# Last experts stage as one stream over its chunks, and shorter gate work in the second merged LSTM and experts stage

## The reference, cut to what matters

```python
z = xz_t + prev_h @ Wh
ai, af, ao, ag = jnp.split(z, 4, axis=1)
next_c = sigmoid(af) * prev_c + sigmoid(ai) * tanh(ag)
next_h = sigmoid(ao) * tanh(next_c)
...
h = jnp.einsum('nc,ech->neh', x_flat, W1) + b1          # 16 experts, top 2
h = _layernorm(h, g1, be1)                              # rsqrt(var + 1e-5)
h = jax.nn.gelu(h, approximate=False)
expert_out = jnp.einsum('neh,eho->neo', h, W2) + b2
```

```python
h = jax.nn.gelu(jnp.einsum('bsd,edf->ebsf', x, W1) + b1[:, None, None, :], approximate=False)
eo = jnp.einsum('ebsf,efd->ebsd', h, W2) + b2[:, None, None, :]
out = jnp.einsum('ebsd,bse->bsd', eo, comb)
x = x + out
```

## Time and profile before

| what | us |
|---|---|
| median of 3 runs (4591.7 to 4593.56) | 4591.94 |
| time of the profiled execution | 4592.8 |
| its span, first to last instruction | 4591.0 |
| merged stage, 160 steps, 1427 to 2163.3 in the trace | 736.3 |
| of it the stretch with experts, 1494 to 2114 | 620 |
| last stage, from 4048.77 to the end | 542.2 |
| mean granted TensorE clock, share of full | 0.963 |

### The profile page before, as it was taken

The page is one execution under the profiler, slowest core; times in us unless marked ns, Lnnn a source line. Parts: engine busy times, 40 slices in busy tenths (PEclk is TensorE's granted clock), DMA queues, the critical chain, the costliest instruction groups (busy, mean ns, idle before and its releaser), DMA issues. The chain is left out here.

```text
span 4591.0 us, 117961 instructions
## 1 busy us (share of the span) xinstructions
PE 4209.4 (92%) x40912; PEld 2942.6 (64%) x40912; DVE 2537.7 (55%) x7670; ACT 1904.5 (41%) x4829; POOL 784.3 (17%) x3251
## 2 busy tenths in 40 slices
PE   6999999999998888898799998999996887889998
PEld 4555776887775455554355887887783555566666
DVE  5775564555554888886555445666666554421111
ACT  4343443333332555564233222666663552333333
POOL 1111221000000666663221000111112110000000
PEclk9999999999999999999799998999998998989999
DMA  1000000000000000000000000000000000000000
GB/s 54 0 0 25 0 0 26 1 0 0 0 0 11 1 2 1 1 1 1 34 0 3 0 0 1 3 3 3 3 3 13 41 0 0 0 1 0 0 0 18
DMA packets 3085, 28.94 MB, mean 6 GB/s; under 512 B 320, under 2 KB 832, under 8 KB 1216
## 3 DMA queue, kind: packets, MB, share of 16 engines
q1 hardware_dynamic: 2768, 24.97, 1.4%
HBM read 22.87 MB, written 2.10 MB: 5 GB/s over the span
## 5 line engine op out<-in xcount | busy, mean ns | idle before, releaser
L2312 DVE SCALAR_TENSOR_TENSOR experts_acc<-banks,experts_gate,experts_acc 128x128 f32<-128x128 f32 x512 | 144.2, 344 | 462.1 <-PE banks L2258 461.0
L2258 PEld LDWEIGHTS banks<-weights,experts_hidden 128*128 128x128 f32 x2560 | 303.3, 192 | 55.0 <-issue 49.7
L604 DVE TENSOR_REDUCE cells_row_max<-banks 128x4 f32<-128x512 f32 x384 | 238.5, 684 | 162.8 <-PE banks L397 162.8
L2258 PE MATMUL banks<-weights,experts_hidden 128*128 128x128 f32 x2560 | 305.2, 275 | 0.0
L2531 ACT ACTIVATE experts_hidden<-banks,weights 128x512 f32<-128x512 f32 x256 | 175.9, 687 | 271.1 <-PE banks L2528 267.2
L761 PE MATMUL banks<-clock_fill 128*128 128x512 bf16 x932 | 282.6, 392 | 1.2 <-PEq L101 1.2
L2528 PE MATMUL banks<-act_a,weights 128*128 (+1 forms) x512 | 263.4, 646 | 0.0
L541 ACT ACTIVATE cells_probs<-banks 128x512 f32<-128x512 f32 x384 | 198.3, 602 | 97.4 <-PE banks L437 90.1
L604 DVE TENSOR_REDUCE attn_row_max<-banks 128x4 f32<-128x512 f32 x256 | 159.0, 684 | 133.4 <-PE banks L397 133.4
L1579 ACT ACTIVATE wave_hidden_turned<-banks,weights 128x128 f32<-128x128 f32 x512 | 205.7, 454 | 40.4 <-PE banks L1523 37.3
L2717 ACT ACTIVATE lin_context_turned<-banks 128x256 f32<-128x256 f32 x128 | 49.2, 384 | 403.7 <-PE banks L2669 403.7
(11 more groups left out here) (528 smaller groups left out, 9909.9 us busy)
## 6 DMA issues: line engine op xcount, KB each, us to landing
weights<-in_p SPq DMA_DIRECT2D x1, 2894.5 KB, 17.2
weights<-in_p SPq DMA_DIRECT2D x1, 2894.0 KB, 9.4
...
x_res<-in_x SPq DMA_DIRECT2D x1, 2048.0 KB, 15.2
out_x<-x_res SPq DMA_DIRECT2D x1, 2048.0 KB, 6.3
...
```

The costliest lines, as they stand in the source:

```text
L604: dve.tensor_reduce(mt[:, 4 * g:4 * g + 4], bank, AX_X, ALU.max).then_inc(s["max_ready"], 1)
L2258: last = pe.matmul(ps[:, 2 + e % 2, t * P:(t + 1) * P], hs[lo:lo + n, (tile + f) % slots, t * P:(t + 1) * P], out_rhs(e, f, lo, n), start= ...
L2312: last = dve.scalar_tensor_tensor(out=acc[:, t, :], in0=ps[:, 2 + e % 2, t * P:(t + 1) * P], scalar=g[:, t, e:e + 1], in1=acc[:, t, :], op ...
```

## The change

The last stage gets a function of its own, `wide_expert_stage`. The sum, the gates and the turned gates have two buffers, by the chunk's parity. The bias is no longer put into the sum ahead of the experts: the first expert writes the sum by a multiply, and a chunk's bias product (one of 128x512 with gates in 128 rows, of which 8 are not zero) and the four products that turn its sum (now plain products with the identity) are added up in one PSUM bank during the next chunk, behind expert 1's output. Gates are turned behind expert 4's output. The hidden tiles of the next chunk's first expert are issued ahead of the last expert's output. The stage's loop takes two chunks in a pass, three times, with the first and last chunk written out. SyncE sends each chunk's 256 KB to memory when it is stored; the block behind the stage is gone.

In the merged stage `guess` is one operation on the bits. The output gate's own operation is gone: `state` is one operation over all 128 rows and 128 columns, (tanh of the gate + 1) times `tc`, where `tc` is now as wide as `hb` and zero off its blocks, so that the cell's tanh is two operations of 64 rows each. The factor 0.5 is in `half_pick`.

```diff
...
-        og, c2, fc, ic, tc = (sb(n, [P, HALF]) for n in ("output_gate", "c_twice", "fc", "ic", "tc"))
-        hb = sb("state_by_batch", [P, P])
+        c2, fc, ic = (sb(n, [P, HALF]) for n in ("c_twice", "fc", "ic"))
+        tc, hb = (sb(n, [P, 2, HALF]) for n in ("tc", "state_by_batch"))
...
-        shifted = sb("variance_shifted", [P, 2, 4], I32)
...
             def turned(st):
                 pe.wait_ge(s["batch_ready"], st.s(1))
-                pe.matmul(ps[:, STATE, 0:2 * NB], hb[:, :], const("half_pick"), start=True, stop=True).then_inc(
+                pe.matmul(ps[:, STATE, 0:2 * NB], hb[:, :, :].rearrange("p h f -> p (h f)"), const("half_pick"), start=True, stop=True).then_inc(
...
             def cell_tanh(st):
                 act.wait_ge(s["c_ready"], st.s(1))
-                act.activation(tc[:, :], c2[:, :], ACT.Tanh, scale=0.5).then_inc(s["tc_ready"], 1)
+                for half in range(2):
+                    rows = slice(half * HALF, (half + 1) * HALF)
+                    last = act.activation(tc[rows, half, :], c2[rows, :], ACT.Tanh, scale=0.5)
+                last.then_inc(s["tc_ready"], 1)
...
-            dve.memset(hb[:, :], 0.0).then_inc(s["c_set"], 1)
+            dve.memset(tc[:, :, :], 0.0).then_inc(s["c_set"], 1)
...
                 dve.scalar_tensor_tensor(out=c2[:, :], in0=fc[:, :], scalar=0.5, in1=ic[:, :], op0=ALU.mult,
                                          op1=ALU.add).then_inc(s["c_ready"], 1)
-                dve.tensor_scalar(og[:, :], th[:, 2, :], 0.5, 0.5, ALU.mult, ALU.add).then_inc(s["gate_ready"], 1)
 
             def state(st):
-                dve.wait_ge(s["gate_ready"], st.s(1))
+
                 dve.wait_ge(s["tc_ready"], st.s(1))
-                for half in range(2):
-                    rows = slice(half * HALF, (half + 1) * HALF)
-                    last = dve.tensor_tensor(hb[rows, rows], tc[rows, :], og[rows, :], ALU.mult)
-                last.then_inc(s["batch_ready"], 1)
+                dve.scalar_tensor_tensor(out=hb[:, :, :], in0=th[:, 2:3, :].broadcast_to([P, 2, HALF]), scalar=1.0,
+                                         in1=tc[:, :, :], op0=ALU.add, op1=ALU.mult).then_inc(s["batch_ready"], 1)
...
             def guess(n, q):
 
                 dve.wait_ge(s["summed"], n + 1)
-                dve.tensor_scalar(shifted[:, q % 2, :], half_var[:, q % 2, :].bitcast(I32), 1, None,
-                                  ALU.logical_shift_right).then_inc(s["shift_ready"], 1)
-                dve.wait_ge(s["shift_ready"], n + 1)
                 past(dve, s["unit_ready"], n - 1)
-                dve.tensor_scalar(inv[:, q % 2, :].bitcast(I32), shifted[:, q % 2, :], -1.0,
+                dve.tensor_scalar(inv[:, q % 2, :].bitcast(I32), half_var[:, q % 2, :].bitcast(I32), -0.5,
                                   float(0x5F3759DF - 0x400000), ALU.mult, ALU.add).then_inc(s["guess_ready"], 1)
...
+def wide_expert_stage(core, out):
+    nc, w, ps, const = core.nc, core.pack(7), core.ps, core.const
+    NE, DEPTH = 8, 4
+    PER = NE * DEPTH
+    OUT, SUM, GTURN = 2, 4, 5
+    gates = core.gate(NE)
+    with stage_scope(nc) as ctx:
+        sb = lambda n, shape: ctx.enter_context(nc.sbuf_tensor(f"experts4_{n}", shape, F32))
+        sem = lambda n: nc.alloc_semaphore("experts4_" + n)
+        hs = sb("hidden", [P, 2 * DEPTH, CHUNK])
+        acc = sb("acc", [P, 2, 4, P])
+        g = sb("gate", [P, 2, 4, NE])
+        gt = sb("gate_turned", [P, 2, CHUNK])
+        s = {n: sem(n) for n in ["set", "g_ready", "gt_done", "gt_ready", "h_done", "h_ready", "y_done", "y_added",
+                                 "sum_done", "stored", "sent"]}
+        block = ctx.enter_context(nc.Block())
+        def chunks(eng, one):
+            one(0, 0, True, False)
+            with eng.Fori(0, NCHUNK // 2 - 1) as i:
+                one(i * 2 + 1, 1, False, False)
+                one(i * 2 + 2, 0, False, False)
+            one(NCHUNK - 1, 1, False, True)
+        @block.sync
+        def _(sp):
+            for c in range(NCHUNK):
+                cols = slice(c * CHUNK, (c + 1) * CHUNK)
+                sp.wait_ge(s["stored"], c + 1)
+                sp.dma_start(out[:, cols], core.x[:, cols]).then_inc(s["sent"], 16)
+            sp.wait_ge(s["sent"], 16 * NCHUNK)
+        @block.gpsimd
+        def _(pool):
+            pool.memset(gt[:, :, :], 0.0).then_inc(s["set"], 1)
+            def one(c, p, first, last):
+                past(pool, s["y_added"], (c - 1) * NE)
+                past(pool, s["gt_done"], c - 1)
+                pool.tensor_copy(g[:, p, :, :], gates[:, bass.ds(c * 4, 4), :]).then_inc(s["g_ready"], 1)
+            chunks(pool, one)
+        @block.tensor
+        def _(pe):
+            wait_pack(pe, core, 7)
+            def hidden(c, e):
+                for f in range(DEPTH):
+                    past(pe, s["h_ready"], c * PER + (e * DEPTH + f - 1))
+                    pe.matmul(ps[:, f % 2, :], w("W1", (e * DEPTH + f) * P, P), core.a[:, tok(c * CHUNK, CHUNK)],
+                              start=True, stop=True).then_inc(s["h_done"], 1)
+            def output(c, e):
+                past(pe, s["y_added"], c * NE + (e - 1))
+                pe.wait_ge(s["h_ready"], c * PER + (e + 1) * DEPTH)
+                for t in range(4):
+                    for f in range(DEPTH):
+                        last = pe.matmul(ps[:, OUT + e % 2, t * P:(t + 1) * P],
+                                         hs[:, e % 2 * DEPTH + f, t * P:(t + 1) * P],
+                                         w("W2", (e * DEPTH + f) * P, P), start=(f == 0), stop=(f == DEPTH - 1))
+                last.then_inc(s["y_done"], 1)
+            def gates_turn(c, p):
+                pe.wait_ge(s["g_ready"], c + 1)
+                past(pe, s["gt_ready"], c)
+                for t in range(4):
+                    last = pe.transpose(ps[0:NE, GTURN, t * P:(t + 1) * P], g[:, p, t, :], const("ident"))
+                last.then_inc(s["gt_done"], 1)
+            def total(c, p):
+                pe.wait_ge(s["y_added"], c * NE + NE)
+                pe.wait_ge(s["gt_ready"], c + 1)
+                past(pe, s["stored"], c)
+                pe.matmul(ps[:, SUM, :], w("b2"), gt[:, p, :], start=True, stop=False, skip_group_check=True)
+                for t in range(4):
+                    last = pe.matmul(ps[:, SUM, t * P:(t + 1) * P], acc[:, p, t, :], const("ident"), start=False,
+                                     stop=True, skip_group_check=True)
+                last.then_inc(s["sum_done"], 1)
+            def one(c, p, first, last):
+                for e in range(NE):
+                    if e + 1 < NE:
+                        hidden(c, e + 1)
+                    elif not last:
+                        hidden(c + 1, 0)
+                    output(c, e)
+                    if e == 1 and not first:
+                        total(c - 1, 1 - p)
+                    if e == 4:
+                        gates_turn(c, p)
+                if last:
+                    total(c, p)
+            hidden(0, 0)
+            chunks(pe, one)
+        @block.scalar
+        def _(act):
+            wait_pack(act, core, 7)
+            act.wait_ge(s["set"], 1)
+            def one(c, p, first, last):
+                for e in range(NE):
+                    past(act, s["y_done"], c * NE + (e - 1))
+                    for f in range(DEPTH):
+                        j = e * DEPTH + f
+                        act.wait_ge(s["h_done"], c * PER + (j + 1))
+                        act.activation(hs[:, e % 2 * DEPTH + f, :], ps[:, f % 2, :], ACT.Gelu,
+                                       bias=w("b1", j, 1)).then_inc(s["h_ready"], 1)
+                    if e == 5:
+                        act.wait_ge(s["gt_done"], c + 1)
+                        past(act, s["sum_done"], c - 1)
+                        act.activation(gt[0:NE, p, :], ps[0:NE, GTURN, :], ACT.Copy).then_inc(s["gt_ready"], 1)
+            chunks(act, one)
+        @block.vector
+        def _(dve):
+            def add(c, p, e):
+                dve.wait_ge(s["y_done"], c * NE + (e + 1))
+                past(dve, s["y_added"], c * NE + e)
+                for t in range(4):
+                    y, gate = ps[:, OUT + e % 2, t * P:(t + 1) * P], g[:, p, t, e:e + 1]
+                    if e == 0:
+                        last = dve.tensor_scalar(acc[:, p, t, :], y, gate, None, ALU.mult)
+                    else:
+                        last = dve.scalar_tensor_tensor(out=acc[:, p, t, :], in0=y, scalar=gate, in1=acc[:, p, t, :],
+                                                        op0=ALU.mult, op1=ALU.add)
+                last.then_inc(s["y_added"], 1)
+            def store(c):
+                dve.wait_ge(s["sum_done"], c + 1)
+                xs = core.x[:, tok(c * CHUNK, CHUNK)]
+                dve.tensor_tensor(xs, ps[:, SUM, :], xs, ALU.add).then_inc(s["stored"], 1)
+            def one(c, p, first, last):
```

(23 more changed lines are left out.)

21 lines of the change are left out of this document (4 added, 17 removed).

## The result

The changed kernel takes 4521.07 us (median, 4516.34 to 4524.8), the one before 4592.75 in the same session: 0.9843, 95% interval [0.9831, 0.9855], 72 us less. Forecast were 4531, 61 less. The profiled execution has a span of 4517.4 us.

The account below looks back on a forecast made before the run. TensorE was taken as the bound, with gaps at the last stage's chunk boundaries and waits for VectorE in the merged stage. Last stage -49 and merged stage -12 make -61, so 4531 us; range 4521 to 4552, own range 4522 to 4541.

Parts of the forecast that it names:

- The bound and the mechanism of the last stage: Last stage: TensorE's work is the bound; without boundary waits the chunks form one stream at full clock, -49 us.
- The start: Last stage's beginning: hidden products start earlier, but at a low clock, which loses 3 us.
- The price of the old restart: Last stage, behind each old chunk boundary: first 16 hidden products take 10.15 us instead of 7.4, up to 2.75 us lost.
- I let 9 us of the 18.1 go: Merged stage, logits steps: 9 us of TensorE's 18.1 us of waits for VectorE's units vanish.
- 4 with the routing and the jump: Merged stage, routing steps and loop's back jump: the shorter guess saves 0.21 us a step, 4 us over some 20 stalls.
- Tanh and state cancel: Merged stage, steps without experts: split tanh +0.16 us (bounds 0.12 and 0.26), single state operation -0.16, sum 0.
- my dear end: Merged stage, cell tanh: the upper bound, +0.26 us, if the two tanh operations don't overlap at all.
- The prediction's second rule: Merged stage, VectorE: an instruction starting in another partition quadrant is held; one state operation gives some 0.08 us more, about 2 in all.
- Rival 1: Last stage: a gap per chunk opens and the clock falls again, costing 19 us, 4550 us; chance 0.15.
- Rival 2: Merged stage gains nothing because TensorE waits for the state's copy; 0 to +4 us, 4543 to 4547; chance 0.20.
- Rival 3: Merged stage: tanh and state lengthen each of 160 steps; kernel slower above 0.36 us a step; chance 0.05 with milder forms.
- The bounds -51 and -18: Cheap ends: last stage -51 us with start and gates cheap, merged stage -18 us with all stalls gone.

Follow-up runs that it names:

- e2: The kernel before with the whole change of the merged stage and the old last stage; 4578.12 us, ratio 0.9968.
- e3: The kernel before with only the guess made one operation on the bits (shift removed); 4572.31 us, ratio 0.9959.
- e6: The changed kernel with serial chunks: each ends with its own total, and TensorE waits for the store before the next chunk's hidden products; 4542.70 us.
- e7: The changed kernel with serial chunks and 6 plus 4 spare TensorE products in the two boundary waits; 4543.52 us.
- e9: The changed kernel with one cell tanh as before and the state as two fused operations of 64 rows; 4530.64 us.
- e13: As e9, with seven more instructions ahead of VectorE's loop in the merged stage (a memset cut into eight); 4517.91 us.
- e4: The kernel before with two tanhs, the folded output gate and one state operation, but the old guess; 4589.22 us, ratio 0.9992.
- e12: As e6, with the gate transposes and ScalarE's copy of them also at the chunk boundary, a third wait; 4558.96 us.

## Why the prediction was right or wrong

**The bound and the mechanism of the last stage: right.** The chunks are one stream at a granted clock of 1.00, with no wait between chunks, as forecast. Two terms were too dear. A chunk lasts 59.75 us and not 60.5 (the pair of 7.27 is the first behind a boundary; further into a chunk the same trace has 7.19, as from 4073.24 to 4080.43; a gate turn costs 59.75 - 8 x 7.19 - 1.75 = 0.5, as forecast), so the last output product ends 480.1 us behind the stage's start, not 485.0. The transfer takes 2.0 and not 3.1, and the tail with it 6.9 and not 8.0. 4.9 + 1.1 = 6.0 make -55.1 of -49. The old stage in the trace of before was a dear one, though: against those of e2 and e3 the gain is some 50, and my 49 would look like a hit with the same two terms wrong.

**The start: right**, 10.15 us from the first hidden product to the first output product, 2.6 us over the 7.53 that e6 shows for the same at the full clock, where I took 3. **The price of the old restart: too high.** I took the 10.15 of one boundary; the seven of before have 9.10 to 10.55, in the mean 9.80.

**"I let 9 us of the 18.1 go", and 4 with the routing and the jump: this step failed.** All but 2.0 went. I sized a logits step from one row, a state of 0.45, and that row lay in the one step of the loop in which the clock had fallen: the state started late enough to miss GpSimd's adds. In 17 others the pair lasted 0.81 to 1.13, beside the adds, and the one operation of the changed kernel lasts at most 0.67 there. A second logits step would have shown it. The routing steps gave 0.26 and 0.30 each (some 4 us, as forecast). The 16.1 us of waits that went are not all of the 21.6: the slow jump step and two slow steps near the stage's start make some 4 more between the two traces. Such steps come and go with the same code (e7, with the changed stage, has a jump step of 7.12 us), so the change can't be credited with them.

**"Tanh and state cancel": right in sum, with two terms wrong.** The pair doesn't overlap (+0.26, my dear end), and the state gives -0.16 as forecast. That would make 0.10 a free step, but the free steps lost 0.03. The missing 0.07 is the output gate's operation with the wait on it, which I had put at nothing because it ran beside the tanh: with it gone the state starts 0.03 behind the tanh and not 0.10, and e9 and e13, which have one tanh and two state operations as before but no gate operation, have free steps of 3.29 for 3.36. The estimate from the Trainium skill's VectorE: DVE Perf Modes, section on the TRN2 errata, 0.24 us for the second tanh, was nearer to the 0.26 than my row of two different operations 0.16 apart. In logits steps the state edit would have paid without the guess (e4: 4.90 for 5.25), but the guess had taken that already: on top of it (e3, 714.07) the stage with both parts (712.65 to 716.10) is the same within its scatter. The prediction's second rule, on an operation of VectorE that starts in another half of the partitions, agrees with the traces. A logits step of the changed kernel:

```profile
1791.69 0.53 DVE L1730 SCALAR_TENSOR_TENSOR wave_state_by_batch<-wave_gates_tanh,wave_tc 128x128 f32<-128x128 f32 x1
1792.15 0.68 DVE L1795 TENSOR_REDUCE wave_half_variance<-wave_square 128x4 f32<-128x516 f32 x1
```

`sums` starts before the state has ended, by 0.08 us in 18 of 104 steps; in before it never starts less than 0.03 behind it.

**Rival 1** (the stream has gaps and the clock falls): didn't come, and its price was wrong. Two missing covers cost 3.1 us a chunk and no clock (e6); with a third wait and the transposes (e12) the clock fell at four of seven boundaries. **Rival 2** (the merged stage doesn't gain): refuted by e2 and e3, which are 12.8 and 18.6 us faster than before. **Rival 3** (slower): the free steps grew by 0.03 us, its point was 0.36.

**The range.** The result lies at its lower end, 4521.07, or by the ratio 0.9843 x 4591.94 = 4519.8, below it. By its own terms the lower end was 4591.9 - 69 = 4522.9. The bounds -51 and -18 were sums of the same rows as the middle, so an atypical row moved all three. And e2's time, 12.8 us for a stage forecast at 12, would have looked like a hit; it was the slower stretches elsewhere, which is luck.
